# Another order of VectorE's slot in pass A of a gated scan with a Fourier layer, and a second scan round of 13 steps

## The reference

```python
mu, var = mean(x), var(x)                        # x: 8 x 2048 x 512
xn = (x - mu) / sqrt(var + 1e-5) * gamma + beta
delta = sigmoid(xn @ w_delta + b_delta)          # 16 states
B_t   = xn @ w_in + b_in
gate  = sigmoid(xn @ w_gate + b_gate)            # 512 columns
h = tanh(h * delta[t] @ A + B_t[t])              # a scan over the 2048 steps
y = (h @ C) * gate + x
x = layernorm(x + y)
x = layernorm(x + (real(ifft(fft(x) @ w)) + bias))
```

## Time and profile before

| | |
|---|---|
| median of 3 runs | 887.87 us (887.8 to 889.6) |
| profiled execution, its own time | 890.39 us |
| span of its trace | 888.6 us |
| mean granted TensorE clock | 0.995 |
| PE busy | 850.6 us (96% of the span) |
| DVE busy | 752.7 us (85%) |
| POOL busy, ACT busy | 576.1 us (65%), 559.7 us (63%) |
| waits of ACT's `hi` for DVE's `xs_sb` in pass A | 165.3 us in 103 waits |
| waits of DVE's `token_pow` for POOL's `mean_square` | 32.7 us in 28 waits |

### The profile page before, as it was taken

One profiled execution on the slowest core, in us unless ns is written; L12 is line 12 of the kernel. 1 busy time (PEld: TensorE's weight loads), 2 busy tenths in 40 slices (PEclk: granted clock), 3 DMA queues, 4 the chain that ended last, 5 costly groups with the idle time before them and its releaser, 6 DMA issues.

```text
span 888.6 us, 16580 instructions
## 1 busy us (share of the span) xinstructions
PE 850.6 (96%) x5074; PEld 455.2 (51%) x5106; DVE 752.7 (85%) x1513; ACT 559.7 (63%) x1066; POOL 576.1 (65%) x906
## 2 busy tenths in 40 slices
PE   8799999999889999999999999999999999999996
PEld 5345455454445555554555555554455555555553
DVE  7878888889999888888789999989878888888883
ACT  5244444543454445444368888888878887888887
POOL 4555556678664555656656666676767776777782
PEclk9999999999999999999999999999999999999998
DMA  8478888777656666777546565657868667767743
GB/s 307 161 267 301 312 309 316 252 268 255 233 195 225 203 204 246 261 254 248 204 150 234 194 235 190 236 195 228 252 226 282 220 237 251 243 231 235 264 163 142
DMA packets 94190, 209.53 MB, mean 236 GB/s; under 512 B 3760, under 2 KB 5040, under 8 KB 90160
## 3 DMA queue, kind: packets, MB, share of 16 engines
q1 hardware_dynamic: 93840, 208.49, 68.7%
q10 hardware_dynamic: 288, 0.27, 0.1%
HBM read 139.53 MB, written 67.11 MB: 233 GB/s over the span
## 4 chain that ended last, share of the span: by engine, by line
PE 62%; DVE 14%; issue 11%; POOL 9%; ACT 3%; DMA 1%; another core or an unknown queue 0%; POOLq 0%; DVEq 0%; ACTq 0%
PE bank L1501 16%; PE bank L1502 16%; PE bank L1504 16%; PE bank L1472 6%; POOL lo_sb L791 5%; PE bank L1657 3%; PE bank L1584 2%; DVE bn L1217 2%; DVE xs_sb L1249 2%; DVE gsum_sb L1264 2%; PE bank L1564 1%; ACT hi_sb L550 1%; DVE zh_sb L1133 1%; DMA x_sb<-x 1%; POOL a_rstd L777 1%
## 5 line engine op out<-in xcount | busy, mean ns | idle before, releaser
L791 POOL TENSOR_TENSOR lo_sb<-xs_sb,hi_sb 128x512 f16<-128x512 f32 x128 | 150.5, 1176 | 148.2 <-ACT hi_sb L550 148.2
L1501 PE MATMUL bank<-wg_hi,hi_sb 128*128 128x512 f16 x508 | 193.1, 380 | 8.4 <-DVE gsum_sb L1264 5.2
L870 POOL TENSOR_TENSOR x_sb<-x_sb,gate_sb 128x512 f32<-128x512 f32 x120 | 153.1, 1276 | 71.9 <-DMA x_sb<-x 57.6
L1501 PE MATMUL bank<-w_re_sb,hi_sb 128*128 128x512 f16 x512 | 194.0, 379 | 2.0 <-DVE w_ring L1375 1.4
L1502 PE MATMUL bank<-w_re_sb,hi_sb 128*128 128x512 f16 x512 | 194.0, 379 | 0.0
L1502 PE MATMUL bank<-wg_lo,hi_sb 128*128 128x512 f16 x508 | 192.8, 379 | 0.0
L550 ACT ACTIVATE hi_sb<-xs_sb 128x512 f16<-128x512 f32 x128 | 80.5, 629 | 168.3 <-DVE xs_sb L1249 165.3
L1504 PE MATMUL bank<-w_re_sb,lo_sb 128*128 128x512 f16 x512 | 131.4, 379 | 0.0
L1504 PE MATMUL bank<-wg_hi,lo_sb 128*128 128x512 f16 x508 | 131.2, 381 | 0.0
L1254 DVE SCALAR_TENSOR_TENSOR lo_sb<-bank,hi_sb 128x512 f16<-128x512 f32 x128 | 88.5, 692 | 49.5 <-ACT hi_sb L710 46.5
L718 ACT ACTIVATE norm_sb<-x_sb,lift_bias,rstd 128x512 f32<-128x512 f32 x128 | 103.1, 806 | 24.3 <-POOL lift_bias L883 23.7
(11 more groups left out here) (198 smaller groups left out, 1341.9 us busy)
## 6 DMA issues: line engine op xcount, KB each, us to landing
x_sb<-x SPq DMA_DIRECT2D x63, 1024.0 KB, 6.4
gate_dram<-gate_sb SPq DMA_DIRECT2D x32, 1024.0 KB, 5.2
out<-out_sb SPq DMA_DIRECT2D x31, 1024.0 KB, 5.3
gate_sb<-gate_dram SPq DMA_DIRECT2D x30, 1024.0 KB, 7.1
out_sb<-x_turned SPq DMA_DIRECT2D x16, 1024.0 KB, 7.3
norm_sb<-x_turned SPq DMA_DIRECT2D x15, 1024.0 KB, 7.3
w_ring<-gate_dram SPq DMA_DIRECT2D x2, 1024.0 KB, 9.6
x_sb<-x SPq DMA_DIRECT2D x2, 512.0 KB, 5.4
```

The source lines that it names most:

```text
L791: pool.tensor_tensor(lo_sb[:, k % 4], xs_sb[:, k % 2], hi_sb[:, k % 4], ALU.subtract).then_inc(s_lo, 1)
L870: pool.tensor_tensor(x_sb[:, k // 4, k % 4], x_sb[:, k // 4, k % 4], gate_tile(n, k), ALU.add).then_inc(s_v, 1)
L1501: nc.tensor.matmul(dst, hi_sb[:, slot_of, t], w_hi[:, t], start=(t == 0), stop=False)
```

## The change

Three things are changed.

1. DVE's slot in pass A is written in another order: `gate_logits(n-1)` first, then `copy_z`, both token steps, the statistics, the scan's product, the wait for the statistics, `scaled(n+2)`, the aggregation, and the rest.
2. Round 1 of either scan group has 13 steps in place of 16 and compares the states of step 12 in each lane; a further round, were it needed, has 16 steps again. The check, its branch and the split of the states move 3 slots forward, and the four splits stand in every second slot.
3. PE's third spread of the token scales comes in slot 6 instead of slot 5.

```diff
+SECOND = 13
+STEPS = CHUNK + SECOND
...
-SCAN_CHECK = tuple(n + 2 * CHUNK for n in SCAN_FIRST)
+SCAN_CHECK = tuple(n + STEPS for n in SCAN_FIRST)
...
+def split_place(n, first):
+
+    return (n - first) // 2 if isinstance(n, int) and n - first in (0, 2, 4, 6) else None
...
-                nc.vector.tensor_copy(ends[rows], last)
+                nc.vector.tensor_copy(ends[rows], h_sb[rows, :, compared::CHUNK])
...
-                if isinstance(n, int) and 1 <= n < 8:
-                    gate_logits(n - 1, n - 1, 0)
...
+                if exists(n - 1):
+                    gate_logits(n - 1, (k - 1) % 8, v if k >= 1 else v - 1)
                 if k == 4 and exists(n - 8):
                     copy_z(v - 1)
                 if k % 4 == 1 and exists(n + 3):
                     token_scale(v * 2 + (k + 3) // 4, (k + 3) // 4 % 2)
+                    token_inverse((k + 3) // 4 % 2)
+                if exists(n + 8) and not (isinstance(n, int) and n < 4):
+                    a_statistics(n + 8, k, v + 1)
+                scan_slot(0, n)
+                if exists(n + 8) and not (isinstance(n, int) and n < 4):
+                    dve.wait_ge(s_bn, n + 9)
                 if exists(n + 2) and not (isinstance(n, int) and n == -1):
                     scaled(n + 2, (k + 2) % 8, v if k < 6 else v + 1)
-                if k % 4 == 1 and exists(n + 3):
-                    token_inverse((k + 3) // 4 % 2)
+                if exists(n + 8) and not (isinstance(n, int) and n < 4):
+                    aggregate(n + 8, k, 8, s_aggr)
+                if isinstance(n, int) and pair_at(n - 1) is not None:
+                    combine(pair_at(n - 1))
+                if k % 4 == 1 and exists(n - 4):
+                    sum_zrow(v if k == 5 else v - 1, 0 if k == 5 else 1)
...
-                elif exists(n + 8):
-                    a_statistics(n + 8, k, v + 1)
-                    dve.wait_ge(s_bn, n + 9)
-                if exists(n - 1) and not (isinstance(n, int) and n < 8):
-                    gate_logits(n - 1, (k - 1) % 8, v if k >= 1 else v - 1)
-                if exists(n + 8) and not (isinstance(n, int) and n < 4):
-                    aggregate(n + 8, k, 8, s_aggr)
-                scan_slot(0, n)
...
-                if isinstance(n, int) and n == 2:
-                    spread_token_scale(1, 1)
-                if k % 4 == 1 and before(n, 2) and exists(n + 3):
+                if isinstance(n, int) and n in (2, 6):
+                    spread_token_scale((n + 2) // 4, (n + 2) // 4 % 2)
+                if k % 4 == 1 and before(n, 6) and exists(n + 3):
```

More of the change, by code:

```diff
@@ L97, in scan_place @@
     j = n - first if isinstance(n, int) else -1
-    return (j // CHUNK, j % CHUNK) if 0 <= j < 2 * CHUNK else None
+    return (j // CHUNK, j % CHUNK) if 0 <= j < STEPS else None
+def split_place(n, first):
+    return (n - first) // 2 if isinstance(n, int) and n - first in (0, 2, 4, 6) else None
 def pair_at(n):
@@ L644, in scan_until_settled @@
                 with act.If(changed > 0):
-                    with act.Fori(2, LANES) as r:
+                    with act.Fori(2, LANES + 1) as r:
                         again = act.value_load(flag[g][0:1, 0:1])
@@ L648, in scan_until_settled @@
                             for s in range(CHUNK):
-                                scan_tanh(g, r * CHUNK + s + 1, s)
+                                scan_tanh(g, r * CHUNK + SECOND - CHUNK + s + 1, s)
                             act.wait_ge(s_flag[g], r)
@@ L666, in split_slot @@
             def split_slot(g, n):
-                if isinstance(n, int) and 0 <= n - SCAN_SPLIT[g] < 4:
-                    state_high(g, n - SCAN_SPLIT[g])
+                if split_place(n, SCAN_SPLIT[g]) is not None:
+                    state_high(g, split_place(n, SCAN_SPLIT[g]))
             def slot(n, k, v):
@@ L1134, in scan_product, with scan_next_round @@
                                         del_sb[rows, :, s + 1::CHUNK], ALU.mult).then_inc(s_hd[g], 1)
-            def scan_next_round(g):
+            def scan_next_round(g, compared):
                 rows = scan_rows(g)
@@ L1146, in scan_next_round, with scan_compare @@
                                         del_sb[rows, :, CHUNK::CHUNK], ALU.mult).then_inc(s_hd[g], 1)
-                nc.vector.tensor_copy(ends[rows], last)
-            def scan_compare(g, r):
+                nc.vector.tensor_copy(ends[rows], h_sb[rows, :, compared::CHUNK])
+            def scan_compare(g, r, compared):
                 rows = scan_rows(g)
-                nc.vector.tensor_tensor(differ[rows], h_sb[rows, :, CHUNK - 1::CHUNK], ends[rows],
+                nc.vector.tensor_tensor(differ[rows], h_sb[rows, :, compared::CHUNK], ends[rows],
                                         ALU.not_equal).then_inc(s_dscan[g], 1)
@@ L1166, in scan_until_settled @@
                 with dve.If(changed > 0):
-                    with dve.Fori(2, LANES) as r:
+                    with dve.Fori(2, LANES + 1) as r:
                         again = dve.value_load(flag[g][0:1, 0:1])
                         with dve.If(again > 0):
-                            scan_next_round(g)
+                            scan_next_round(g, CHUNK - 1)
                             for s in range(CHUNK):
-                                dve.wait_ge(s_h[g], r * CHUNK + s + 1)
+                                dve.wait_ge(s_h[g], r * CHUNK + SECOND - CHUNK + s + 1)
                                 if s + 1 < CHUNK:
                                     scan_product(g, s)
-                            scan_compare(g, r)
+                            scan_compare(g, r, CHUNK - 1)
                             scan_flag(g, r)
@@ L1194, in scan_slot @@
                     dve.wait_ge(s_h[g], r * CHUNK + s + 1)
-                    if s + 1 < CHUNK:
+                    if s + 1 < (CHUNK, SECOND)[r]:
                         scan_product(g, s)
                     elif r == 0:
-                        scan_next_round(g)
+                        scan_next_round(g, SECOND - 1)
                     else:
-                        scan_compare(g, 1)
+                        scan_compare(g, 1, SECOND - 1)
                 if isinstance(n, int) and n == SCAN_CHECK[g] + 1:
@@ L1204, in split_slot @@
             def split_slot(g, n):
-                if isinstance(n, int) and 0 <= n - SCAN_SPLIT[g] < 4:
-                    state_low(g, n - SCAN_SPLIT[g])
+                if split_place(n, SCAN_SPLIT[g]) is not None:
+                    state_low(g, split_place(n, SCAN_SPLIT[g]))
             def aggregate(n, k, ring, aggr_done):
@@ L1595, in scan_until_settled @@
                 with pe.If(changed > 0):
-                    with pe.Fori(2, LANES) as r:
+                    with pe.Fori(2, LANES + 1) as r:
                         again = pe.value_load(flag[g][0:1, 0:1])
@@ L1599, in scan_until_settled @@
                             for s in range(CHUNK):
-                                scan_step(g, r * CHUNK + s + 1, s)
+                                scan_step(g, r * CHUNK + SECOND - CHUNK + s + 1, s)
                             count_changes(g, r)
```

## The result

The changed kernel takes 954.11 us (median of 4 runs, 952.05 to 957.04), the kernel before 888.13 on the same chip (4 runs, 887.8 to 889.6): ratio 1.0742, 95% interval 1.0707 to 1.0777. The profiled execution of after has a span of 953.8 us against 888.6.

What follows compares the result with a forecast made beforehand. PE, 96% busy, bounds the kernel before; a DVE-ACT ring of 3.33 us a slot bounds it after. 35.3 + 1.1 + 12.7 + 11.9 - 1.5 + 6 = +65.5 us, so 953 us; 8 in 10: 928 to 978.

Steps and rivals of the forecast that it cites:

- The ring: Pass A: logits, statistics, scaling, ACT's high half and sigmoid, then next logits, 3.33 us a slot, over PE's 2.81.
- The token steps: Slots with k = 1 and 5: DVE waits for the low half and `token_pow`, +0.78 us each.
- the term for the copy of z: Slots with k = 4: `copy_z` on DVE adds 0.55 us.
- Slots 8 to 61: Pass A before the scan, 54 slots at 3.33 us plus additions: 196.8 against 161.58 us, +35.3.
- The clock: PE's slow products after long pauses, 21 quads outside the scan: 0 to 25 us possible, 6 taken.
- The pauses: PE stands about 2.8 us before each spread of the token scales, in one piece, once a quad.
- the rival of 972 us: The clock falls in every quad: 25 us instead of 6, so 972 us; chance 0.08.
- The scan: Slots 70 to 98, 29 slots at 3.95 us plus additions: 122.8 against 110.1 us, +12.7.
- the product in the ring: Slots 70 to 98: scan's product, 0.74 us, adds 0.62 a slot as the statistics' wait is over; bounds 0.5 to 0.74.
- Slots 99 to 119: Pass A after the scan, 21 slots at 3.33 us plus additions and splits: 81.2 against 69.3 us, +11.9.
- The splits: Slots 99 to 119: four state splits, high half 0.54 and low half 0.68 us, follow the sigmoid; 4.9 us.
- The steps: Six scan steps fewer, at most 0.63 us of PE each; three in pass B give 1.0 to 1.9: -1.5 us.

Runs made afterwards that it cites:

- run 3: Changed kernel with ACT's sigmoid of tile n-2 put ahead of the high half of tile n+2 in each slot: 908.15 us, 1.021 to the kernel before.
- run 6: Changed kernel with DVE's wait for its own statistics moved from ahead of the scaling to behind it: 942.55 us, 1.0616 to the kernel before.
- run 5: Changed kernel with PE's transpose of the projections and spread of token scales behind the product in slots with k = 2 or 6: 950.12 us.
- run 7: Changed kernel with PE's third spread of the token scales back in slot 5: 953.87 us, 1.0732 to the kernel before.
- run 1: Kernel before with only the 13-step second rounds and the spread-out splits, DVE's order and PE's spread unchanged: 884.78 us, 0.9948.
- run 4: Changed kernel with DVE's scaling moved ahead of the statistics and the scan's product: 927.1 us, 1.0442 to the kernel before.

## Why the prediction was right, and where its terms were not

- **The ring** is the cause, as predicted. It was read off two slots of before at 3.33 us and is 3.36 in slot 46. Opened on ACT (run 3) it gives back 46 us, shortened by one wait (run 6) 11.6. The token steps are right too (4.11 us in slots with k = 1 and 5 behind the loop); the term for the copy of z was 0.16 too small (slots with k = 4 take 4.22, with k = 0 3.51, so 0.71 and not 0.55).
- **Slots 8 to 61, 9.6 more than predicted.** The step that failed is that one slot's hand-overs hold for all: the slots of the earlier trace rows are written out, and 32 of the 54 stand in a loop, where the octets are 30.55 long instead of 29.07. With 0.4 for each octet behind the loop that is 203.8, and run 5 took 203.87 with the clock at 1.00.
- **The clock.** Taken at 6, found at 5.2: 2.5, 0.4 and 2.3 us in slots 8 to 61, 62 to 69 and 99 to 119 between after and run 5, and 4.0 in the medians (in the scan run 5 was 2.1 slower). The slots by which after is longer there are those behind the pauses that slow matmuls followed (10, 18, 26, 34, 50, 62, 102, 110 and 118: 0.4 to 0.8 us each, 1.4 in slot 102); behind the one that ends in slot 37 nothing is lost, and pauses without slow matmuls cost nothing that shows. The pauses themselves are longer than the 2.8 us that were read, up to 3.5; the prediction's own figures (14.3 to 14.8 less 11.2) make 3.1 to 3.6. And half of their time in slots 8 to 61 ends with `zrow`, not with the diagonal (21.2 and 19.7 us). One of them in the granted clock (stretches of after, of PE the matmuls and loads of L1506 alone):

```profile
119.00:121.00 2.00, 0.00 (x0) 0.00 (x0) 1.00 0.00 0
121.00:122.00 1.00, 0.44 (x1) 0.16 (x2) 0.61 0.00 0
122.00:124.00 2.00, 1.47 (x3) 0.45 (x3) 0.50 0.71 259
```

and two in PE's timeline:

```profile
106.12 0.38 PE L1506 MATMUL bank<-wg_hi,hi_sb 128*128 128x512 f16 x1 [2.69 <-POOL diag L793]
...
121.13 0.64 PE L1583 MATMUL bank<-cst,zrow 128*128 128x128 f32 x2 [3.39 <-DVE zrow L1286]
121.56 0.63 PE L1506 MATMUL bank<-wg_hi,hi_sb 128*128 128x512 f16 x1
```

Behind 3.39 us of waiting the clock went to 0.50 (1.2 GHz) and matmuls to 0.63 us, behind 2.69 it stayed. Of the 20 waits of 2 us and more on PE's matmuls in pass A from slot 8 on, 11 were followed by slow matmuls (2.68 to 3.51 us) and 9 not (2.05 to 3.28); in run 7 two waits of 3.88 us were not. So the length of a wait alone does not tell whether the clock falls. A slow product does shorten the next pause: in slots 8 to 39 of after and run 7 the diagonal is waited for 3.88 us behind a product at full speed and 2.68 to 2.69 behind a slow one. The Trainium skill, "TensorE: Matmul & The Clock Gate" (HAM oscillation), tells of a loop that falls back in every pass, with longer waits than most of these; here it was somewhat over half of them, and the rival of 972 us was rightly small.
- **The scan, +4.9 instead of +12.7.** The term mis-sized is the product in the ring: it was to add 0.62 us a slot (0.74 less the 0.12 of the statistics' own wait, with bounds of 0.5 and 0.74) and adds 0.15 (slot 75 takes 3.51, slot 46 3.36). DVE's timeline of after in slot 75:

```profile
308.74 0.68 DVE L1224 BATCH_NORM_STATS2 bn<-x_sb 128x6 f32<-128x512 f32 x1
309.34 0.36 DVE L1140 TENSOR_TENSOR zh_sb<-h_sb,del_sb 64x128 f32<-64x128 f32 x1
309.63 0.68 DVE L1256 TENSOR_TENSOR xs_sb<-out_sb,bank 128x512 f32<-128x512 f32 x1
```

From start to start the product takes 0.29, and the scaling behind it no longer waits for the statistics. Over 29 slots that is 13.6 us less than predicted; the scan is only 7.8 under its term, because single slots are longer than the ring (slot 85, in which the round changes, takes 5.28, slot 94 4.52), for which the prediction had no term.

The 0.74 of the earlier trace rows was not the product's own time, but the end of an instruction of POOL. In the trace of before 21 of the 30 products that it shows in pass A started well inside one; they took 0.61 to 1.31 us, and each ended 0.23 to 0.26 behind it. The other nine took 0.34 to 0.40, and were there to be read. In the new order the product mostly starts when POOL is idle or within 0.05 us of its end (24 of 28).
- **Slots 99 to 119, 3.1 more than predicted.** The splits came out as worked (+4.9 over their slots). 2.3 of the 3.1 are the clock, 1.4 of that in slot 102; most of the rest is the ring (3.36 for 3.33) and the copy of z. The branch behind the check stands in that slot too, and costs nothing that shows: in run 5, with the same branch, slot 102 takes 3.37 us, like any other. In after it takes 4.77, and its end waits for a product of slow matmuls:

```profile
416.34 0.63 PE L1506 MATMUL bank<-wg_hi,hi_sb 128*128 128x512 f16 x1
...
420.05 0.75 DVE L1271 SCALAR_TENSOR_TENSOR gsum_sb<-bank,row_factor,gbias_sb 128x512 f32<-128x512 f32 x1 [1.77 <-PE bank L1509]
```

- **The steps**: -1.5 was too little; pass B is 3.0 shorter here and 4.4 in run 1, a microsecond and more for each step left out where I had 0.63 of PE as the most. Why so much more was not tried. That 13 suffice, that the spread is worth nothing and that start and end of pass A hardly move was right.

So the mechanism was right, and the sum was right partly by chance: the ring of slots 8 to 61 was taken 7 us too small, the scan 7.8 too large.

## What to carry to other kernels

Before an operation is put ahead of its neighbours on one engine, follow what it needs round through the other engines back to itself: two buffers and an in-order queue make a ring of it, and as long as nothing else ends later, every start-to-start time on that ring is paid in each pass, however idle the engines are. Read the length of a ring from a slot of the same kind (in the loop, not beside it). And where one instruction shows several durations in a trace, look at what runs on its neighbour engine before the mean is moved to another place.

## What the runs showed of the hardware

An instruction of VectorE with two operands in SBUF and one of GpSimd hold each other up. In pass A of all twelve kernels every product of the scan (120 of them) that began more than 0.05 us behind the start of an instruction of GpSimd and more than 0.07 ahead of its end ended 0.22 to 0.27 us behind it, whatever its own start (0.36 to 1.31 us in all), and every other took 0.34 to 0.42. The second instruction of `sum_zrow`, with both tiles in SBUF too, took 0.29 alone and 0.94 in run 4, where it ended 0.15 behind GpSimd. It also goes the other way: in the nine cases of before and run 1 where the product began at most 0.05 us behind GpSimd's low half, the product took 0.34 to 0.36, and the low half 1.38 to 1.42 instead of 1.16. Statistics (one operand in SBUF) and logits (one of the two tiles in PSUM) do not change: 0.66 to 0.70 us and 0.71 to 0.76. The Trainium skill, "SBUF — State Buffer" (Who interferes with whom), says that the two engines share a pair of ports under an exclusive lock, and that a VectorE instruction with two SBUF inputs contends with a GpSimd instruction that reads SBUF; these traces agree. I had not brought that to the rows of before.

Hand-overs on a semaphore cost more in the loop of slots 8 to 39, whose waits stand against registers, than in the slots written out behind it: in after and run 5 0.78 to 0.97 us from the statistics to the scaling (0.84 in the mean) against 0.69 to 0.73, and 0.72 to 0.82 from there to ACT against 0.72. Whether the registers or something else of the loop makes the difference was not tried.
